# The first of four layers written as one unrolled, software-pipelined program instead of a loop over pairs of batches

## The chip, the cores and the metric

One core of a Trainium2 chip. The metric is the device time of one execution in microseconds (us), median of several runs.

## The reference

Eight batches of 512 tokens with 128 channels pass through four layers: a Performer layer (attention by random features, and a feed-forward part), a rotary causal attention layer with a mixture of experts, a second attention layer, and a routed feed-forward layer. Only the first is touched here. With a layer norm before it and a residual after it, it computes for each batch:

```python
q, k, v = split(video @ Wq.T + bq), split(video @ Wk.T + bk), split(video @ Wv.T + bv)   # 16 heads of 8
# features of q and k, xp = (x * norm) @ proj.T, 32 a head:
#   ratio * (exp(xp - diag - stab) + EPS_K); stab is the maximum over a token's features (queries)
#   or over all tokens and features of the head (keys); diag is half the squared length, scaled
k_sum = jnp.sum(kp, axis=2)
denom = jnp.einsum('bhnm,bhm->bhn', qp, k_sum)
ctx = jnp.einsum('bhnm,bhnd->bhmd', kp, v)
out = jnp.einsum('bhnm,bhmd->bhnd', qp, ctx) / denom[..., None]
x = layer_norm(video + out @ Wo.T + bo, g2, be2)
return layer_norm(x + relu(x @ W1.T + b1) @ W2.T + b2, g3, be3)
```

## The kernel before

Every tensor of a batch lies with 128 tokens on the partitions, as four tiles (T = 4), or transposed with channels on the partitions. The whole X (8 batches) stays in SBUF. The function performer_layer writes one program for each engine, and semaphores join them. The programs are loops over four steps (the last step is written out behind a loop of three), and a step handles two batches, the lanes L = 0 and 1. Each lane owns four of the eight PSUM banks.

A step goes in this order, each part for both lanes before the next: y (the normalised input) is transposed and multiplied by wq, wk and wv; ScalarE (ACT) keeps q and k and their squares; PE sums the squares (hsel) to half lengths, which are transposed to dg. The keys' features are multiplied out tile by tile (L508, L518); VectorE (DVE) takes the maximum of each head (L329), and ACT copies the tile from PSUM to kp in SBUF (L443). GpSimd (POOL) takes the maximum over the partitions with partition_all_reduce (L251). The queries' features (L525) get their maxima (L340), the shift (L349) and the exponential (L448). Then the keys in SBUF are shifted (L358) and exponentiated (L451). EPS_K is added to both by POOL for lane 0 (L257, L261) and by DVE for lane 1 (L292). PE forms contexts and key sums with 32-column products on four groups of columns (L538), turns the queries' features, and multiplies (L561). DVE divides (reciprocal L370, product L372), adds the residual, norms (L72, L76, L78, L101) with the inverse root on POOL (L239), scale and shift (L314, L316); feed-forward products L576 and L581; two more norms. DVE writes all four normalisations itself (L101, L302).

In the loop the waits are against registers, and some instructions are preceded by a semaphore increment of passed that carries the wait:

```python
pool.wait_ge(km_ready[L], i + 1)
pool.sem_inc(passed, 1)
nc.gpsimd.partition_all_reduce(stab[L][:], km[L][:], P, RMAX).then_inc(stab_ready[L], 1)
```

SyncE issues the layer's loads and 65 writes of pads that a later layer needs. The next layer's first loads and its work begin when all engines have left this layer's block.

Of the kernel before, what the change touches and what calls it, by code (L numbers as in the profile page):

```python
# [18 lines left out]
M = 32  # L19
# [111 lines left out]
def performer_layer(nc, X, ident, w, consts, padded):  # L131


    ctx = ExitStack()
    with ctx:
        sems = []

        def sem(name):
# [4 lines left out]
        sb2 = lambda name, shape, dt=F32: [sb(f"{name}{L}", shape, dt) for L in range(LANES)]  # L143
        sem2 = lambda name: [sem(f"{name}{L}") for L in range(LANES)]

        banks = [[ctx.enter_context(nc.psum_tensor(f"pf_bank{L}{i}", [P, 512], F32)) for i in range(4)]
                 for L in range(LANES)]

        wq, wk, wv, wo = (sb(n, [P, D]) for n in ("wq", "wk", "wv", "wo"))
        w1 = sb("w1", [P, F])  # L150
        w2 = sb("w2", [P, FC, D])
        bq, bk = sb("bq", [P, 1]), sb("bk", [P, 1])
        b1 = sb("b1", [P, FC])
        bv, bo, b2, g2, be2, g3, be3 = (sb(n, [P, D]) for n in ("bv", "bo", "b2", "g2", "be2", "g3", "be3"))
        feats = sb("feats", [P, H * M])
        hsel = sb("hsel", [P, 32])
        bmask = sb("bmask", [P, P])
        ones = sb("ones", [P, 32])
        half = sb("half", [P, T])
        stats, mv, rstd = sb2("stats", [P, T, 6]), sb2("mv", [P, T, 2]), sb2("rstd", [P, T])  # L160
        y, yb, yT = sb2("y", [P, T, D]), sb2("yb", [P, T, D]), sb2("yT", [P, S])
        qT, kT, sqq, sqk = (sb2(n, [P, S]) for n in ("qT", "kT", "sqq", "sqk"))
        v = sb2("v", [P, T, D])
        dgT, dg = sb2("dgT", [64, S]), sb2("dg", [P, T, 64])
        kmx, km, stab = sb2("kmx", [P, T, H]), sb2("km", [P, H]), sb2("stab", [P, H])
        ck, qmx, cq = sb2("ck", [P, T, H]), sb2("qmx", [P, T, H]), sb2("cq", [P, T, H])
        kp, qp = sb2("kp", [P, T, H * M]), sb2("qp", [P, T, H * M])
        cm, cx = sb2("cm", [P, 2, P]), sb2("cx", [P, 2, P])
        qpT = sb2("qpT", [P, T, S])
        rd, oT = sb2("rd", [P, S]), sb2("oT", [P, S])  # L170
        r, x1, x1b, x1T = sb2("r", [P, T, D]), sb2("x1", [P, T, D]), sb2("x1b", [P, T, D]), sb2("x1T", [P, S])
# [30 lines left out]
        def ahead(i):  # L202

            return 0 if isinstance(i, int) else 1

        def steps(eng, body):

            with eng.Fori(0, STEPS - 1) as i:
                body(i)
# [2460 lines left out]
```

## Time and profile before

| | |
|---|---|
| median of 3 runs | 1964.24 us (1961.62 to 1968.32) |
| the profiled execution's own time | 1969.18 us |
| its span | 1967.4 us |
| mean granted TensorE clock over the span | 0.873 of full |
| PE, DVE, ACT, POOL busy | 78%, 69%, 51%, 39% of the span |

The profile is one execution of the program. PE is the matmul engine, PEld its weight loads. Busy shares are over the whole span, of which the first layer is about a fifth; a row about a stage is read from the trace with a window. A matmul of 32-bit operands leaves two records.

### The profile page before, as it was taken

Reading aid. Unit: us, or ns where it says so; the run is one execution under the profiler, and the core shown is the slowest. Engines: PE = TensorE matmul, PEld = TensorE weight load, DVE = VectorE, ACT = ScalarE, POOL = GpSimd, SP = SyncE. Lnnn points to the kernel's source line nnn. Section 1 sums busy time; section 2 is a strip of 40 time slices with the busy share of each in tenths; the row PEclk is TensorE's granted clock in tenths of the full one; section 3 lists DMA queues with packets and bytes.
Section 4 is the critical chain, followed back from the end, with each engine's and each line's share of the span. In section 5 each row is a group of like instructions: output and inputs, shape, how many; then the busy total and the mean of one; then the engine's idle time right before and its main releaser. Section 6 shows DMA issues by size and latency. Waiting matters only on the chain. (4 is left out here: it accounts for less than half of the span.)

```text
span 1967.4 us, 26210 instructions
## 1 busy us (share of the span) xinstructions
PE 1537.9 (78%) x8477; PEld 972.8 (49%) x8477; DVE 1349.8 (69%) x3332; ACT 993.9 (51%) x1645; POOL 758.6 (39%) x871
## 2 busy tenths in 40 slices
PE   5475757537999999968737999999999478699990
PEld 2343434324666666633314555555554456577770
DVE  4557676746677777725867777887784465588874
ACT  3232323211565666532442667777776434477772
POOL 1121222214455555332555112212200357488875
PEclk9687878765899999978966999999999589799995
DMA  7500000013222222100006543444440011344424
GB/s 227 197 0 0 0 0 0 1 37 93 68 68 70 70 70 70 33 12 0 1 6 159 133 111 90 121 123 122 116 96 14 23 51 47 117 134 127 133 62 129
DMA packets 96189, 144.20 MB, mean 73 GB/s; under 512 B 31138, under 2 KB 59939, under 8 KB 91952
## 3 DMA queue, kind: packets, MB, share of 16 engines
q1 hardware_dynamic: 91072, 134.18, 24.3%
q0 software_dynamic: 4992, 8.48, 1.3%
q8 instruction: 63, 1.03, 0.2%
q14 instruction: 62, 0.51, 0.1%
HBM read 104.25 MB, written 57.48 MB: 82 GB/s over the span
## 5 line engine op out<-in xcount | busy, mean ns | idle before, releaser
L1010 DVE TENSOR_REDUCE ctx_nm<-ctx_s 128x1 f32<-128x512 f32 x512 | 329.5, 681 | 95.1 <-PE ctx_s L1286 94.4
L1122 ACT ACTIVATE ctx_probs<-ctx_st 128x1024 f32<-128x1024 f32 x256 | 254.2, 1022 | 113.6 <-PE ctx_st L1302 109.3
L1010 DVE TENSOR_REDUCE rope_nm<-rope_s 128x1 f32<-128x128 f32 (+3 forms) x512 | 230.4, 481 | 88.1 <-PE rope_s L1289 85.6
L1122 ACT ACTIVATE rope_probs<-rope_st 128x1024 f32<-128x1024 f32 (+1 forms) x256 | 172.3, 702 | 141.4 <-PE rope_st L1302 140.4
L1286 PE MATMUL ctx_s<-ctx_kst,ctx_qst 96*128 96x512 f32 x512 | 219.7, 467 | 17.2 <-DMA ctx_kst<-ctx_contexts 8.2
L1286 PE MATMUL rope_s<-rope_kst,rope_qst 96*128 96x128 f32 (+3 forms) x512 | 186.2, 396 | 4.4 <-DVE rope_nm L1010 3.6
L1302 PE MATMUL ctx_st<-ctx_qst,ctx_kst 98*128 98x512 f32 x512 | 164.7, 404 | 2.3 <-ACT ctx_probs L1122 2.3
L1286 PEld LDWEIGHTS ctx_s<-ctx_kst,ctx_qst 96*128 96x128 f32 x512 | 100.3, 196 | 131.0 <-DVE ctx_nm L1010 54.9
L875 POOL TENSOR_SCALAR_AFFINE_SELECT rope_probs<-rope_probs 128x256 f32<-128x256 f32 x256 | 98.3, 409 | 172.5 <-ACT rope_probs L1122 172.0
L1302 PE MATMUL rope_st<-rope_qst,rope_kst 98*128 98x512 f32 (+3 forms) x512 | 141.7, 360 | 3.9 <-ACT rope_probs L1122 3.9
L2476 DVE TENSOR_TENSOR sw_hf<-sw_silu,sw_u 128x512 f32<-128x512 f32 x124 | 84.6, 682 | 85.5 <-ACT sw_silu L2246 52.6
L2246 ACT ACTIVATE sw_silu<-sw_g 128x512 f32<-128x512 f32 x124 | 74.2, 598 | 121.0 <-PE sw_g L109 96.4
L2482 DVE TENSOR_TENSOR sw_hl<-sw_hf,sw_hh 128x512 fp32r<-128x512 f32 x124 | 128.6, 1037 | 0.1
L1318 PE MATMUL ctx_out<-ctx_probs,ctx_vaug 128*32 128x512 f32 x1024 | 123.8, 602 | 0.2 <-ACT ctx_probs L1122 0.2
L1286 PEld LDWEIGHTS rope_s<-rope_kst,rope_qst 96*128 96x128 f32 x512 | 104.4, 204 | 34.5 <-issue 17.6
L1289 PE MATMUL rope_s<-rope_maskb,rope_identb 128*128 128x128 bf16 x512 | 120.6, 240 | 0.0
L2335 POOL DMA_INDIRECT sw_ys<-sw_yo,sw_xin x92 | 104.2, 1132 | 29.1 <-issue 23.8
L1302 PEld LDWEIGHTS ctx_st<-ctx_qst,ctx_kst 98*128 98x128 f32 x512 | 97.7, 193 | 24.0 <-ACT ctx_probs L1122 6.9
L239 POOL TENSOR_TENSOR pf_rstd<-pf_mv,pf_half 128x4 f32<-128x4 f32 x32 | 33.0, 1031 | 194.9 <-DVE pf_mv L78 194.9
L1302 PEld LDWEIGHTS rope_st<-rope_qst,rope_kst 98*128 98x128 f32 x512 | 92.3, 201 | 14.4 <-ACT rope_probs L1122 5.9
L2318 POOL TENSOR_TENSOR sw_wl<-sw_raw,sw_wh 128x1536 fp32r<-128x1536 f32 x24 | 84.1, 3504 | 36.7 <-ACT sw_wh L2224 36.7
L1318 PE MATMUL rope_out<-rope_probs,rope_vaug 128*32 128x512 f32 (+3 forms) x1024 | 84.4, 449 | 3.0 <-POOL rope_probs L875 3.0
(380 smaller groups left out, 3346.8 us busy)
## 6 DMA issues: line engine op xcount, KB each, us to landing
sw_raw<-in_L_ffn_all SPq DMA_DIRECT2D x24, 768.0 KB
sw_xs<-in_pad SPq DMA_DIRECT2D x65, 260.0 KB, 9.4
rope_halves<-rope_qk SPq DMA_DIRECT2D x24, 512.0 KB
ctx_halves<-ctx_qk SPq DMA_DIRECT2D x24, 512.0 KB, 6.0
ctx_qst<-ctx_contexts SPq DMA_DIRECT2D x32, 384.0 KB
ctx_kst<-ctx_contexts SPq DMA_DIRECT2D x32, 384.0 KB
rope_qst<-rope_halves SPq DMA_DIRECT2D x32, 192.0 KB
rope_kst<-rope_halves SPq DMA_DIRECT2D x32, 192.0 KB
```

Of the source, the lines that this page charges most:

```text
L875: last = nc.gpsimd.affine_select(blocks, blocks, [[0, 2], [1, P]], compare_op=ALU.is_ge, fill=0.0, base=0, channel_multiplier=-1)
L1010: nc.vector.tensor_reduce(nm[:, g, j * T + t:j * T + t + 1], bank("s", b, n)[:, 0:keys], AXX, ALU.max, negate=True).then_inc(s_used, 1)
L1122: nc.scalar.activation(probs[n // GH % 2][:, n % GH, u * units[0]:u * units[0] + units[u]], st_bank[u][:, 0:units[u]], ACT.Exp, scale=SCAL ...
L1286: last = nc.tensor.matmul(out[:, 0:keys], qst[0:KS, g, j, t * P:(t + 1) * P], kst[0:KS, g, j, 0:keys], start=True, stop=not causal)
L1289: last = nc.tensor.matmul(out[:, keys - P:keys], identb[:], maskb[:], start=False, stop=True)
L1302: last = nc.tensor.matmul(st_bank[u][:, lo:lo + width[c]], kst[:, g, j, c * P:(c + 1) * P], qst[:, g, j, S - width[c]:S], start=True, stop ...
L1318: last = nc.tensor.matmul(o_bank[32 * j:32 * j + 32, S - width[c]:S], vaug[g // 2][:, s, c, j, :], probs[s][:, j, at(c):at(c) + width[c]], ...
L2246: nc.scalar.activation(silu[m % 2][:], g_bank[m % 2][:], ACT.Silu).then_inc(silu_ready, 1)
L2318: nc.gpsimd.tensor_tensor(wl[s % WR][:], raw[s % 2][:], wh[s % WR][:].bitcast(F32), ALU.subtract).then_inc(wl_ready, 1)
L2335: nc.gpsimd.indirect_dma_start(ys[:, :], bass.IndirectOffsetOnAxis(ap=where_to, axis=0), yo[j % YR][:, t, :], None, bounds_check=2 * B * S ...
L2476: nc.vector.tensor_tensor(hf[m % 3][:], silu[m % 2][:], u_bank[m % 2][:], ALU.mult).then_inc(hf_ready, 1)
L2482: nc.vector.tensor_tensor(hl[m % RING][:], hf[m % 3][:], hh[m % RING][:].bitcast(F32), ALU.subtract).then_inc(hl_ready, 1)
```

## The change

The loop over pairs of batches becomes a straight program over 13 rounds. In round b the engines work on different stages of up to six batches: main part m = b, input part f = b+1, input norm f2 = b+2, division and first norm a = b-1, feed-forward e = b-2, last two norms g = b-3. Most buffers are single or doubled rings. Eight PSUM banks are divided anew: four (held) keep a batch's key features from the product to the shift, so that the shift reads PSUM and writes kp (no copy by ACT), and serve between for the contexts, numerator, denominator and both feed-forward products; two rings of two (brief) serve all else, each claimed in an order fixed by IN_ROUND. The keys' and queries' EPS_K and ratio leave the elementwise work: queries' by the bias of the copy out of PSUM, keys' by extra products of v with a constant tile floor and by EPS_K * S in the mask. v's bias moves into mask_contexts. The four normalisations move to ACT (scale and bias operands, whose bias nb is a small DVE operation, offsets); the scales and shifts by g2, be2, g3, be3 and the squares of q and k move to POOL. The reciprocal and its product (divide) of batch b-1 stand on DVE behind the first two maxima of the keys of batch b.

Core of the diff (removed lines are in the kernel printed above):

```diff
+        held = [ctx.enter_context(nc.psum_tensor(f"pf_held{k}", [P, 512], F32)) for k in range(T)]
+        RB = 2
+        brief = {who: [ctx.enter_context(nc.psum_tensor(f"pf_{who}{k}", [P, 512], F32)) for k in range(RB)] for who in ("dve", "act")}
+        rounds = range(-2, B + 3)
+        IN_ROUND = {"dve": [("wo", 1, 1), ("qx", 0, T)],
+                    "act": [("x1T", 2, 1), ("yT", -1, 1), ("q", -1, 1), ("k", -1, 1), ("v", -1, 1), ("dg", -1, 1), ("dgt", -1, 1),
+                            ("qpT", 0, T), ("cx", 0, 1)]}
+        FOR_W2, FOR_CM, FOR_NUM, FOR_DEN = range(4)
...
+            def key_features(m, t):                                   # PE
...
+                if t == FOR_W2 and m >= 3:
+                    pe.wait_ge(r2_ready, m - 2)
+                if t == FOR_CM and m:
+                    pe.wait_ge(cm_ready, m)
+                if t == FOR_NUM and m:
+                    pe.wait_ge(oT_ready, m)
+                if t == FOR_DEN and m:
+                    pe.wait_ge(rd_ready, m)
+                nc.tensor.matmul(held[t][:], tile(kT[m % 2], t), feats[:], start=True, stop=True).then_inc(kx_ps, 1)
...
+            def contexts(m):
...
+                for t in range(T):
+                    for g in range(4):
+                        nc.tensor.matmul(dst[32 * g:32 * g + 32, 0:P], left(t, g), kp[:, t, g * P:(g + 1) * P], start=t == 0, stop=False)
+                        nc.tensor.matmul(dst[32 * g:32 * g + 32, 0:P], left(t, g), floor[:], start=False, stop=t == T - 1)
+                for t in range(T):
+                    for g in range(4):
+                        last = nc.tensor.matmul(dst[32 * g:32 * g + 32, P:2 * P], ones[:], kp[:, t, g * P:(g + 1) * P], start=t == 0, stop=t == T - 1)
...
+            def widen(e):
+                pe.wait_ge(x1T_ready, e + 1)
+                for c in range(FC):
+                    if e + 2 < B:
+                        pe.wait_ge(kx_used, (e + 2) * T + c + 1)
...
+                    nc.tensor.matmul(held[c][:], tile(w1, c), x1T[:], start=True, stop=True).then_inc(h_ps, 1)
...
+            # PE's round: key_features 0, 1; turn_x1(e); turn_input(f); key_features 2, 3; output(a); query_features 0, 1;
+            # project(f); query_features 2, 3; widen(e); lengths(f); turn_lengths(f); contexts(m); turn_queries(m);
+            # turn_contexts(m); narrow(e); attend(m)
...
+            def largest_key(m):                                       # POOL
+                pool.wait_ge(km_ready, m + 1)
+                nc.gpsimd.partition_all_reduce(stab[:], km[:], P, RMAX).then_inc(stab_ready, 1)
...
+            for b in rounds:
+                m, f, f2, a, g = b, b + 1, b + 2, b - 1, b - 3
+                if within(m):
+                    largest_key(m)
+                if within(g):
+                    inverse_root(2, g)
+                if within(f):
+                    squares(f)
+                if within(g):
+                    affine2(g)
+                if within(a):
+                    inverse_root(1, a)
+                if within(f2):
+                    inverse_root(0, f2)
+                if within(g):
+                    inverse_root(3, g)
+                if within(a):
+                    affine1(a)
+                if within(f2):
+                    with_bias(f2)
...
+            def offsets(k, c):                                        # DVE
+                dve.wait_ge(rstd_ready[k], c + 1)
+                nc.vector.scalar_tensor_tensor(nb[k][:, c], mv[k][:, c, :, 0], -1.0, rstd[k][:, c], ALU.mult, ALU.mult).then_inc(nb_ready[k], 1)
...
+            def divide(a):
+                dve.wait_ge(nd_ps, 2 * a + 2)
+                nc.vector.reciprocal(rd[:], held[FOR_DEN][:]).then_inc(rd_ready, 1)
+                dve.wait_ge(rd_ready, a + 1)
+                if a:
+                    dve.wait_ge(wo_ps, a)
+                nc.vector.tensor_tensor(oT[:], held[FOR_NUM][:], rd[:], ALU.mult).then_inc(oT_ready, 1)
...
+            def shift_keys(m):
+                dve.wait_ge(stab_ready, m + 1)
...
+                    nc.vector.tensor_tensor(feat(kp[:, t, :]), feat(held[t][:]), each(ck[:, t, :], M), ALU.subtract).then_inc(kx_used, 1)
...
+            # DVE's round: with_x1(g); largest_keys(m) 0, 1; divide(a); spread(2); largest_keys(m) 2, 3; moments(2);
+            # with_input(a); shift_queries(m, 0); offsets(2); shift_keys(m); spread(1); shift_queries(m, 1); moments(1);
+            # spread(0, f2); offsets(1); moments(0); spread(3); offsets(0); mask_contexts(m); moments(3); offsets(3); residual(g)
...
+            # ACT's round: keep_x1(e); keep_input(f); keep_projected(f); query_exponents(m, 0); normalise(2, g);
+            # key_exponents(m); rectify(e); query_exponents(m, 1); keep_lengths(f); place_lengths(f); input_norm(f2);
+            # keep_queries(m); normalise(1, a); keep_contexts(m); normalise(3, g)
```

In the diff the three rounds that stand here as comments are written as calls, in that order. spread is the statistics (bn_stats) of four tiles, moments their aggregation and the addition of EPS. claim on PE waits until the bank two claims earlier in the same ring has been emptied.

## Rows read from the trace of the kernel before

**Rows 1.** Timeline, where the first layer starts and ends: start, duration, instructions [idle before].
```profile
5.58 0.87 DVE L72 BATCH_NORM_STATS2 pf_stats<-X 128x6 f32<-128x128 f32 x4 [5.58 <-PEq L2572]
...
15.50 1.28 ACT L431 ACT_TABLE_LOAD   x1 [15.50 <-DMA pf_bv<-in_L_attn_bv]
...
428.96 1.29 DVE L405 TENSOR_TENSOR X<-X,pf_r 128x512 f32<-128x512 f32 x2
```

**Rows 2.** Windows, third step: length, busy of PE, PEld, DVE, ACT, POOL, clock, DMA.
```profile
210.76:309.93 99.17, 61.64 (x382) 37.43 (x381) 67.92 (x166) 30.53 (x46) 21.80 (x17) 0.81 0.00 0
```

**Rows 3.** Waits of DVE, then of PE, in the same step: us, times, longest.
```profile
DVE pf_r L390 <- PE pf_bank L581: 9.4, 2, 6.5
DVE pf_dg L324 <- PE pf_bank L513: 5.5, 1, 5.5
...
PE pf_bank L508 <- DVE pf_v L320: 10.6, 1, 10.6
```

**Rows 4.** Lines by form, DVE, 0 to 430.3 us; L349, L72, L76 also by timeline.
```profile
L370 DVE RECIPROCAL pf_rd<-pf_bank 128x512 f32<-128x512 f32 x8 | 26.8, 3353 | 17.1 <-PE pf_bank L561 17.1
L101 DVE TENSOR_SCALAR pf_x<-pf_r,pf_mv,pf_rstd 128x128 f32<-128x128 f32 x64 | 17.8, 342 | 1.7 <-POOL pf_rstd L239 1.7
L314 DVE TENSOR_TENSOR pf_x<-pf_x,pf_g 128x512 f32<-128x512 f32 x16 | 11.0, 689 | 0.3
...
249.68 2.48 DVE L349 TENSOR_TENSOR pf_qp<-pf_bank,pf_cq 128x512 f32<-128x512 f32 x4
...
423.49 0.86 DVE L72 BATCH_NORM_STATS2 pf_stats<-pf_x 128x6 f32<-128x128 f32 x4
424.50 0.38 DVE L76 BATCH_NORM_AGGREGATE pf_mv<-pf_stats 128x2 f32<-128x6 f32 x4 [0.15 <-DVE pf_stats L72]
```

**Rows 5.** Timeline, ACT and POOL: single instructions that carry the sums.
```profile
151.47 2.25 ACT L448 ACTIVATE pf_qp<-pf_qp 128x1024 f32<-128x1024 f32 x2 [4.60 <-DVE pf_qp L349]
...
227.41 2.47 POOL L246 TENSOR_TENSOR pf_yb<-pf_y,pf_bo 128x512 f32<-128x512 f32 x2
...
302.43 4.15 ACT L470 ACTIVATE pf_hT<-pf_bank,pf_b 128x512 f32<-128x512 f32 x7 [2.69 <-PE pf_bank L576]
...
426.67 1.03 POOL L239 TENSOR_TENSOR pf_rstd<-pf_mv,pf_half 128x4 f32<-128x4 f32 x1 [0.50 <-DVE pf_mv L78]
...
440.90 1.65 ACT L1082 ACTIVATE Y<-X,rope_nb,rope_rstd 128x128 f32<-128x128 f32 x4 [33.07 <-DMA rope_bv<-in_L_ffn_bv]
```

**Rows 6.** Timeline around the all-reduce: steps 1 and 2, and its end in step 4.
```profile
37.48 0.42 DVE L333 TENSOR_REDUCE pf_km<-pf_kmx 128x16 f32<-128x64 f32 x2
49.21 0.78 POOL L251 PARTITION_ALL_REDUCE pf_stab<-pf_km  x2 [20.51 <-issue]
61.22 1.04 POOL L257 TENSOR_SCALAR pf_qp<-pf_qp 128x1024 f32<-128x1024 f32 x1 [11.23 <-issue]
...
146.16 0.42 DVE L333 TENSOR_REDUCE pf_km<-pf_kmx 128x16 f32<-128x64 f32 x2
152.52 0.78 POOL L251 PARTITION_ALL_REDUCE pf_stab<-pf_km  x2 [22.73 <-issue]
160.00 2.15 POOL L257 TENSOR_SCALAR pf_qp<-pf_qp 128x1024 f32<-128x1024 f32 x2 [6.70 <-issue]
...
358.58 4.21 POOL L257 TENSOR_SCALAR pf_qp<-pf_qp 128x1024 f32<-128x1024 f32 x2 [6.97 <-ACT pf_qp L448]
```

**Rows 7.** Timeline of PE in the third step.
```profile
233.35 5.53 PE L508 MATMUL pf_bank<-pf_feats,pf_kT 128*128 128x512 f32 x8 [10.61 <-DVE pf_v L320]
244.88 3.60 PE L525 MATMUL pf_bank<-pf_feats,pf_qT 128*128 128x512 f32 x8
268.80 1.08 PE L538 MATMUL pf_bank<-pf_kp,pf_v 128*32 128x128 f32 x32 [1.13 <-POOL pf_kp L261]
```

**Rows 8.** Windows of the L508 and the L525 work of rows 7.
```profile
233.00:239.00 6.00, 5.65 (x11) 2.38 (x12) 0.80 (x2) 0.00 (x0) 0.00 (x0) 0.66 0.00 0
245.00:250.00 5.00, 3.47 (x9) 1.21 (x7) 3.97 (x10) 1.14 (x2) 0.00 (x0) 1.00 0.00 0
```

More of the change, by code:

```diff
@@ L156, in performer_layer @@
[L156 to L165, printed above, removed]
@@ new lines, in shift_queries @@
+            def shift_queries(m, pair):
+                for t in (2 * pair, 2 * pair + 1):
+                    dve.wait_ge(qx_ps, m * T + t + 1)
+                    last = nc.vector.tensor_reduce(qmx[:, t, :], feat(bank("qx", m, t)[:]), AXX, ALU.max)
+                ch.do(last)
+                ch.sync()
+                dve.wait_ge(dg_ready, m + 1)
+                ch.do(nc.vector.tensor_tensor(cq[:, both(pair)], qmx[:, both(pair)], dg[m % 2][:, both(pair), 0:H], ALU.add))
+                ch.sync()
+                for t in (2 * pair, 2 * pair + 1):
+                    if m and t == 0:
+                        dve.wait_ge(qpT_ps, m * T)
+                    nc.vector.tensor_tensor(feat(qp[:, t, :]), feat(bank("qx", m, t)[:]), each(cq[:, t, :], M), ALU.subtract).then_inc(qx_used, 1)
@@ new lines, in residual @@
+            def residual(g):
+                dve.wait_ge(n3_ready, g + 1)
+                x = X[:, g * T:(g + 1) * T, :]
+                nc.vector.tensor_tensor(x, x, x3[:], ALU.add).then_inc(done, 1)
+            for b in rounds:
+                m, f2, a, g = b, b + 2, b - 1, b - 3
+                if b == -1:
+                    dve.wait_ge(projected, 16 * H)
+                    nc.vector.tensor_scalar_mul(feats[:], feats[:], DH ** -0.25).then_inc(feats_ready, 1)
+                if within(g):
+                    with_x1(g)
+                if within(m):
+                    largest_keys(m, (0, 1))
+                if within(a):
+                    divide(a)
+                if within(g):
+                    spread(2, r2)
+                if within(m):
+                    largest_keys(m, (2, 3))
+                if within(g):
+                    moments(2, g)
+                if within(a):
+                    with_input(a)
+                if within(m):
+                    shift_queries(m, 0)
+                if within(g):
+                    offsets(2, g)
+                if within(m):
+                    shift_keys(m)
+                if within(a):
+                    spread(1, r)
+                if within(m):
+                    shift_queries(m, 1)
+                if within(a):
+                    moments(1, a)
+                if within(f2):
+                    if f2 == LANES:
+                        dve.wait_ge(x_loaded, 16)
+                    spread(0, X[:, f2 * T:(f2 + 1) * T, :])
+                if within(a):
+                    offsets(1, a)
+                if within(f2):
+                    moments(0, f2)
+                if within(g):
+                    dve.wait_ge(x2_ready, g + 1)
+                    spread(3, x2)
+                if within(f2):
+                    offsets(0, f2)
+                if within(m):
+                    mask_contexts(m)
+                if within(g):
+                    moments(3, g)
+                    offsets(3, g)
+                    residual(g)
```

726 lines of the change are left out of this document (368 added, 358 removed).

## The prediction

> **What bounds the kernel now.** I read the page first: four layers stand one behind another in the span, and the diff touches only the first (all names with pf_). The timeline's ends give its place: its first DVE instruction starts at 5.58 us, its weights let ACT and PE start at 15.50, its last residual starts at 428.96 and ends at 430.25 [rows 1]. The rest of the span, 1,537 us, runs the same code before and after; the change moves it to an earlier or later start and nothing else, as the next layer's loads start only when this one has ended. So the sum is made for 430.3 us.
>
> Next the windows: a step of the loop (two batches) lasts 99.2 us; DVE is busy for 67.9 of them, PE 61.6, ACT 30.5, POOL 21.8, the granted clock 0.81 [rows 2]. No engine is full. The table of waits says why: DVE waits 9.4 us for the second feed-forward product and 5.5 for the lengths; PE waits 10.6 us for DVE before the key features [rows 3]. The two batches of a step move in lock step through a chain DVE to PE to ACT, and where one engine works the others stand. The bound is latency, 49.6 us a batch, with DVE as the largest worker (34.0 a batch).
>
> **What the change does to each engine's work.** Per batch in the new program:
>
> DVE. A 512-wide operation that reads PSUM takes 0.69 us, and four in a row 2.48, so 0.62 apiece. There are 20 (four key maxima, four query maxima, eight shifts, oT, the sums with_input, with_x1 and residual): 12.4. Reciprocal 3.35. Sixteen statistics at 0.28 alone, four in 0.86: 3.4; sixteen aggregates (four in 0.38) 1.5; and sixteen small ones (masks, epsilon, offsets, sums over heads), for which I take 0.2 each, between a 0.1 aggregate and a 0.28 statistic: 3.1. Sum 23.8 us [rows 4]. Gone are the affine pairs (their first halves alone took 11.0 us over eight batches), all four normalisations (two of them 17.8), the two additions of EPS_K over 2048 columns, v's bias and the copy of dg [rows 4]: 34.0 becomes 23.8.
>
> ACT. It inherits the normalisations: the next layer's own one, four instructions of 128 columns, takes 1.65 us; four of them 6.6. Sixteen copies and Relus of 0.6 to 0.7 make 9.7, four exponentials of 1024 columns 4.2 [rows 5]. About 20.6 us: not a bound.
>
> POOL. Four inverse roots of 1.03, and eight 512-wide sums and products of 1.25 (squares two, affine1 three, affine2 two, yb one): 14.2 us [rows 5]. Then the all-reduce, and here the rows say more than its 0.43 us. In the second step the key maxima end at 146.58, the two all-reduces start at 152.52 and end at 153.30, 6 us after the first maximum although POOL had been idle for 22.7 us, and the second costs only 0.4 more: a fixed price in front. The next POOL instruction had its data from ACT since 152.6 and starts at 160.00, 6.7 us after the all-reduces. In the fourth step the way back is 7.0; in the first the two gaps are 11.5 and 11.2 [rows 6], while SyncE's queue was issuing the pads. So going to the all-reduce costs about 6.1 us and coming back about 6.8. The Trainium skill (GPSIMD Engine Reference, 2.1 Instruction dispatch) says that the first call to a freshly loaded Q7 kernel pays a code load of about 6 us that has no instruction in the profile; by that page alone one load for each change of library would cost what the row shows, and it speaks against this change, which makes eight such trips instead of four. In the sum: POOL 14.2+0.4+6.1+6.8 = 27.5 us a batch, now the largest worker.
>
> PE. At full clock a 512-column product costs 0.85 (eight records of the query features in 3.60 with the last one's tail) [rows 7]. Sixteen of them (features 8, projections 2, widen 4, attention 8 that run four at a time and cost 2) are 13.7; the 128-column products, four in 0.86: v, wo and four groups of narrow, 5.2; seven groups of four transposes 3.0; hsel 0.9; contexts 0.9 for v and 0.9 for ones. The new products with floor repeat v's: 0.9 if four column groups still overlap. About 25.5 us.
>
> **The round, which sets the time.** No worker fills 49.6, so I walk one steady round (b from 3 to 7), from T = 0, when divide has written oT of batch b-1. Each step is a duration above. Held bank 2 is free: key product 2 to 1.1, product 3 to 2.0, their maxima to 2.7, km at 3.0. The all-reduce runs at once if its code is already loaded: stab 3.5. POOL comes back at 10.2, inverse_root(2) ends 11.3. DVE meanwhile does moments(2), with_input, shift_queries(0) to 7.7, and then stands in offsets(2) until 11.3: a new stall of 3.6 us, since that small operation is queued before shift_keys, whose stab has long been there. POOL's round begins with the wait for km, and behind it are queued inverse_root(2), squares(f), on which PE's lengths and contexts wait, and all other roots. No DMA is added or moved on any queue. shift_keys to 14.1, shift_queries(1) to 17.6. PE waits with widen for each shifted key tile, to 15.9; ACT's rectify and second query exponent to 18.7, dgT and dg behind them 20.3, contexts on PE from 19.8 to 22.5. The masks to 23.5, moments(3), POOL and offsets(3) to 25.3. ACT has the input norm to 23.0, four qpT copies 25.5, normalise(1) 27.2, cx 27.6, normalise(3) 29.3, so residual ends at 30.0. PE ends narrow at 29.5 and attend at 31.3. The next round: key products 0 and 1 to 33.1, the second maximum 33.7, reciprocal and oT 37.8, which is the next T. The reciprocals' move costs nothing by itself: after the first two maxima DVE has nothing else that is ready, and the next key products wait for the banks that divide empties.
>
> So 38 us a round at full clock. PE stands still for 4 us at the divide; before, after 10.6 us of standing four key products took 5.53 us and four query products, after work without a gap, 3.60 [rows 7]; the granted clock was 0.66 (part at 1.2 GHz, part at 2.4) in the stretch with the first and 1.00 in that with the second [rows 8]. I add 1.5: 39.5. POOL is idle from 32.4 and its load for the next all-reduce (6.1) ends at 38.5, before the next km at 42.5: hidden.
>
> Ends. The pads' traffic stays. Round 0 starts at 20.5 as before; its km comes about 28.5, POOL is back 11.2 later [rows 6], its squares(1) hold PE's contexts(0): T of round 1 about 58. Rounds 1 and 2 have no third norm and last 29 each: 116. Five rounds of 39.5: 314. The drain has no key work: output, norm 1, widen and narrow of batch 7, its two last norms behind those of batch 6, in DVE's order: about 42. The layer ends at 356 instead of 430.3: 74 us less. The profiled execution took 1969.2 (span 1967.4), 5 above the median of 1964.2; the difference is the same for both, so 1964-74 = 1890.
>
> **Rivals.**
> (a) The code load waits with the all-reduce. The rows can't exclude it: before, a signal stood between wait and all-reduce, and the load ran behind it; in the new program nothing does, so I take the load as free to run early. If it isn't, stab and all behind it come 6.1 us later in each round that has one, and POOL's return moves to 17.3, so DVE stalls nearly 10 us in offsets(2): 5 times 6.1 and some 7 in rounds 1 and 2, 37 us: 1927.
> (b) The products with floor don't overlap. Each stands directly behind the product with the same 32 columns of the array; before, neighbours were always on other columns, and 32 records took 1.08 us [rows 7], no row shows the new order. If the next column group starts only with the last of four passes of 0.107 (a quarter of a 512-column record), 16 pairs take 5.1 in place of 1.8, some 3.3 to 4.2 us a round on the path contexts, masks, norm 3: 8 rounds, 30 us: 1920. The Trainium skill (TensorE: Matmul & The Clock Gate, Part 3, The mechanism) says that matmuls are a strict queue without reordering; by it this case would hold, though the trace's L538 rows show two passes of each product overlapping in fours.
> (c) It is slower. Each all-reduce pays the first step's price, 11.5 and 11.2, fully on DVE's path: a round is 38+6.1+9.8 = 54, and 130+5x54+42 = 442, 12 us later: 1976. It decides from 51 a round. Against it: the second and the fourth step show 6.7 and 7.0 back [rows 6], and the fourth is straight-line code as the new program is.
> (d) It packs better: the drain overlaps, rounds of 36: 1865.
>
> **Numbers.** The forecast 0.62 (my range 1870 to 1910), (a) 0.14, (b) 0.13, (c) 0.04, (d) 0.07. The walk has some 40 hand-offs, each perhaps 0.1 late, so errors lean up: the range is 1860 to 1930. A measurement here tells 0.3% (6 us) from no change. Faster 0.94, same 0.02, slower 0.04.
>
> **What would show it.** The last pf residual near 356. DVE's wait in offsets(2) for POOL of 3 to 4 us in rounds 3 to 7 (about 10: rival a), with the all-reduce within 1 us of km. POOL's next instruction 6.8 us after each all-reduce. L538's successor, 64 records for v and floor, in 2 us (5 or more: rival b). Reciprocals without PE waiting long before them. The forecast is wrong if POOL's return is not hidden at all or doesn't happen, or if ACT's strict order (four norms between the copies) holds qpT back.

## The result and the profile after

On the chip that timed both, the changed kernel took 1942.11 us (median of 4 runs, 1934.17 to 1942.89) beside 1965.24 (1961.62 to 1968.32) for the kernel before: ratio 0.9874, 95% interval 0.9843 to 0.9905. So it is faster, by 1.3%, which is clear of the 0.3% that a measurement tells from no change, and outside the predicted range: the forecast had 74 us, of which 23 came, a third.

The layer's end is the sharper measure, since the rest of the program runs unchanged code, and that rest is not constant: it took 1537.2 us in the profile before and 1527.6 in the one after, so that 9.5 of the 35.0 us between the two spans have nothing to do with the layer. Timeline of DVE, its last line in the layer:

```profile
404.09 0.69 DVE L578 TENSOR_TENSOR X<-X,pf_x 128x512 f32<-128x512 f32 x1 [1.71 <-ACT pf_x L636]
```

It ends at 404.78 instead of 430.25 [rows 1]: 25.5 us earlier, where 356 was forecast; 48.8 us are missing. Timeline of POOL, the eight all-reduces (one a round), which give the rounds' length:

```profile
46.62 0.39 POOL L419 PARTITION_ALL_REDUCE pf_stab<-pf_km  x1 [11.11 <-issue]
84.06 0.40 POOL L419 PARTITION_ALL_REDUCE pf_stab<-pf_km  x1 [17.78 <-DVE pf_km L520]
121.36 0.40 POOL L419 PARTITION_ALL_REDUCE pf_stab<-pf_km  x1 [10.16 <-DVE pf_km L520]
157.26 0.40 POOL L419 PARTITION_ALL_REDUCE pf_stab<-pf_km  x1 [10.15 <-DVE pf_km L520]
201.75 0.39 POOL L419 PARTITION_ALL_REDUCE pf_stab<-pf_km  x1 [10.06 <-DVE pf_km L520]
245.99 0.40 POOL L419 PARTITION_ALL_REDUCE pf_stab<-pf_km  x1 [10.06 <-DVE pf_km L520]
290.19 0.40 POOL L419 PARTITION_ALL_REDUCE pf_stab<-pf_km  x1 [10.06 <-DVE pf_km L520]
332.26 0.40 POOL L419 PARTITION_ALL_REDUCE pf_stab<-pf_km  x1 [10.83 <-DVE pf_km L520]
```

The forecast had the first at 28.5, the next three at 61, 90 and 119, then one every 39.5, and 79 from the last to the end. So the first is 18.1 us late, the next three intervals (37.4, 37.3, 35.9) are 4.9, 8.3 and 6.9 too long, the four steady ones (44.5, 44.2, 44.2, 42.1) 17.0 together, and the tail (72.5) is 6.5 short: 48.7. Five places, then, not one.

Windows of one steady round (length, busy of PE, PEld, DVE, ACT, POOL, clock), which answers to [rows 2] for half a step:

```profile
201.75:245.99 44.24, 33.57 (x224) 19.16 (x224) 26.08 (x70) 19.61 (x36) 14.41 (x13) 0.85 0.00 1
```

The work of three engines came near the forecast (in brackets): ACT 19.6 (20.6), POOL 14.4 (14.2 and 0.4), DVE 26.1 (23.8). PE's 33.6 are well above the 25.5 that I had at full clock; the clock was 0.85 here, and a round of the best version below, at 1.00, has 28.7. No engine is full all the same, and what was furthest off is the waiting. Waits from 215 to 262, which answer to [rows 3]:

```profile
POOL pf_rstd L415 <- issue: 7.0, 1, 7.0
DVE pf_nb L501 <- POOL pf_rstd L415: 5.6, 4, 3.8
...
PE pf_held L362 <- DVE pf_kp L530: 4.4, 1, 4.4
...
PE pf_held L263 <- DVE pf_oT L509: 3.9, 1, 3.9
```

Timeline of DVE in that round; the lines of [rows 6] are answered by 245.59 here, 245.99 above and 253.36 below:

```profile
232.16 1.41 DVE L578 TENSOR_TENSOR X<-X,pf_x 128x512 f32<-128x512 f32 x1 [4.07 <-ACT pf_x L636]
233.50 0.68 DVE L572 TENSOR_TENSOR pf_r<-pf_held,pf_x1b 128x512 f32<-128x512 f32 x1
235.52 1.48 DVE L514 TENSOR_REDUCE pf_kmx<-pf_held 128x16 f32<-128x512 f32 x2 [1.35 <-PE pf_held L263]
236.92 3.35 DVE L505 RECIPROCAL pf_rd<-pf_held 128x512 f32<-128x512 f32 x1
240.30 0.69 DVE L509 TENSOR_TENSOR pf_oT<-pf_held,pf_rd 128x512 f32<-128x512 f32 x1
...
245.59 0.26 DVE L520 TENSOR_REDUCE pf_km<-pf_kmx 128x16 f32<-128x64 f32 x1
...
254.45 1.01 DVE L501 SCALAR_TENSOR_TENSOR pf_nb<-pf_mv,pf_rstd 128x4 f32<-128x4 f32 x1 [3.76 <-POOL pf_rstd L415]
255.38 1.14 DVE L525 TENSOR_TENSOR pf_ck<-pf_dg,pf_stab 128x64 f32<-128x64 f32 x1
256.56 2.48 DVE L530 TENSOR_TENSOR pf_kp<-pf_held,pf_ck 128x512 f32<-128x512 f32 x4
```

The same stretch on POOL:

```profile
231.75 1.28 POOL L440 TENSOR_TENSOR pf_x<-pf_x,pf_be 128x512 f32<-128x512 f32 x1
...
253.36 1.05 POOL L415 TENSOR_TENSOR pf_rstd<-pf_mv,pf_half 128x4 f32<-128x4 f32 x1 [6.98 <-issue]
254.41 1.03 POOL L426 TENSOR_TENSOR pf_sqq<-pf_qT 128x512 f32<-128x512 f32 x1
255.41 1.03 POOL L426 TENSOR_TENSOR pf_sqk<-pf_kT 128x512 f32<-128x512 f32 x1
257.22 1.27 POOL L448 TENSOR_TENSOR pf_x<-pf_x,pf_g 128x512 f32<-128x512 f32 x1 [0.78 <-ACT pf_x L636]
```

And on PE:

```profile
213.37 6.49 PE L362 MATMUL pf_held<-pf_x1T,pf_w 128*128 128x512 f32 x8 [4.66 <-DVE pf_kp L530]
...
222.51 0.45 PE L309 MATMUL pf_held<-pf_kp,pf_v 128*32 128x128 f32 x8
222.75 0.42 PE L310 MATMUL pf_held<-pf_floor,pf_v 128*32 128x128 f32 x8
...
224.28 1.13 PE L313 MATMUL pf_held<-pf_kp,pf_ones 128*32 128x128 f32 x32
...
234.32 1.96 PE L263 MATMUL pf_held<-pf_feats,pf_kT 128*128 128x512 f32 x4 [0.19 <-DVE pf_r L572]
...
241.05 3.78 PE L263 MATMUL pf_held<-pf_feats,pf_kT 128*128 128x512 f32 x4 [3.90 <-DVE pf_oT L509]
```

Read together: the all-reduce starts 0.14 us after km has ended, so nothing was left to load in between (the code that the all-reduce needs, called its library below), and POOL's next instruction starts 6.98 us behind it; DVE waits 3.76 in offsets(2). All three were forecast. Not forecast: two key products take 1.96 us at 234.32 and 3.78 at 241.05, behind 3.90 us of standing; eight records of widen take 6.49 behind 4.66 us of standing, where eight of the query features took 3.60 [rows 7]; and three DVE operations (1.41, 1.01, 1.14) take two to six times what they take elsewhere in the layer (0.69, 0.16, 0.22).

Each ratio below has the kernel before timed beside it (1952.6 to 1953.8 there), with its 95% interval. A steady round is half the distance between km or the all-reduce of batch 4 and batch 6; in the changed kernel 44.2.

A layer end is read from one profile, and it is only good to some 6 us. Two kernels below ("keys shifted before offsets(2)" and "both moves") have the changed kernel's code in every round up to the all-reduce of batch 3. It starts at 157.26 us in the changed kernel, at 160.21 in the first of them, and in the second at

```profile
163.17 0.39 POOL L419 PARTITION_ALL_REDUCE pf_stab<-pf_km  x1 [9.86 <-DVE pf_km L520]
```

The load ahead of the first all-reduce took 11.1, 10.9 and 13.7 us in the three, and the way back from it 10.4, 12.5 and 12.2. So a gain of a few us counts only where it arises behind the edit, in rows that the edit explains; the 22 to 35 us of the copy, the divide first and the maximum by PE stand clear of this.

### The profile page after: what moved, and what is told of

It is laid out like the page before. It is cut to its first block and busy times, and to the rows that moved or that the text cites. A ratio compares the mean times of both kernels' runs of the same rounds, so it can differ in the third digit from the quotient of the medians.

```text
span 1932.4 us, 26699 instructions
## 1 busy us (share of the span) xinstructions
PE 1551.3 (80%) x8728; PEld 973.5 (50%) x8733; DVE 1282.8 (66%) x3212; ACT 1026.0 (53%) x1747; POOL 792.7 (41%) x909
## 5 line engine op out<-in xcount | busy, mean ns | idle before, releaser
L1444 PEld LDWEIGHTS rope_s<-rope_kst,rope_qst 96*128 96x128 f32 x512 | 103.7, 203 | 33.6 <-issue 16.9
L2485 POOL DMA_INDIRECT sw_xs<-sw_rows,sw_slots x64 | 66.9, 1046 | 47.0 <-issue 35.6
```

Of the source, the lines that this page charges most:

```text
L1444: last = nc.tensor.matmul(out[:, 0:keys], qst[0:KS, g, j, t * P:(t + 1) * P], kst[0:KS, g, j, 0:keys], start=True, stop=not causal)
```

## Experiments

**A copy for the all-reduce.** A copy of km on POOL replaces it, so the maximum over the partitions is left out.

```diff
-                nc.gpsimd.partition_all_reduce(stab[:], km[:], P, RMAX).then_inc(stab_ready, 1)
+                nc.gpsimd.tensor_copy(stab[:], km[:]).then_inc(stab_ready, 1)
```

> The changed kernel with a plain copy of km to stab in place of the all-reduce: the maximum over the partitions is left out. Theory 1 (the way back from the all-reduce, 7.0 us with 10.4 in round 0, holds offsets(2) and squares on POOL, and DVE and PE behind them): POOL's next operation follows within 0.2 us, DVE's wait of 3.8 us in offsets(2) is gone, a steady round falls from 44.2 to about 39, the first rounds lose some 17 and twice 3 us, in all 45 to 55 us less than the changed kernel. Theory 2 (the round is set by hand-offs and PE's clock, POOL's pause is mostly hidden): only the first round's 17 us and under 1 us a round, so 17 to 25 us less.

Ratio 0.9673 (0.9641 to 0.9704), layer end 369.46, steady round 38.6. Timeline of POOL:

```profile
223.24 0.20 POOL L419 COPY pf_stab<-pf_km 128x16 f32<-128x16 f32 x1 [9.78 <-DVE pf_km L520]
223.75 1.02 POOL L415 TENSOR_TENSOR pf_rstd<-pf_mv,pf_half 128x4 f32<-128x4 f32 x1 [0.31 <-DVE pf_mv L497]
```

The 6.98 us behind the all-reduce are gone. The trips cost the layer 35.3 us: 11.7 up to the maximum of batch 1; 5.0, 6.5, 4.8 and 3.0 in the four intervals after batch 3 (5.6 in the steady round); and 4.8 in the tail. Not all of it is DVE's wait: with POOL back early, widen follows without a gap and takes 3.60 us, and ck takes 0.21. The intervals between batches 1, 2 and 3 hardly move (37.6 and 36.1 beside 37.3 and 35.9), so the loads are not what is wrong there.

**The same copy in the kernel before**, the maximum over partitions left out again.

> The kernel before with plain copies of km to stab in place of the all-reduces: the maximum over the partitions is left out. Theory 1 (before, the code loads lay beside the queries' exponents, which come at the same time): a step stays at 99.2 us within 1, only the first step gains its cold load, the layer ends 5 to 12 us earlier, so that the loads of the changed kernel (35 us there) are a cost that the change itself put on the path. Theory 2 (they were on the path before too): each step loses 6 us or more, the layer ends 25 us or more earlier.

Ratio 0.9983 (0.9968 to 0.9997), layer end 428.41: 1.8 us earlier. That is a net of two parts. The keys' maxima of step 2 end 8.8 us earlier (137.75 beside 146.58), but the two steps behind them take 103.9 and 102.4 us instead of 99.5 and 99.0, where theory 1 had them unchanged; TensorE was busy for 66.3 us of the first of these instead of 61.7, at a clock of 0.77 instead of 0.79, and why is open. What the run does show is that taking the all-reduces out brought next to nothing before and brings 35 us now. Timeline of POOL in step 2, its first instruction behind the two copies:

```profile
143.97 1.04 POOL L257 TENSOR_SCALAR pf_qp<-pf_qp 128x1024 f32<-128x1024 f32 x1 [5.86 <-ACT pf_qp L448]
```

Even with nothing to come back from, POOL stands for 5.86 us until ACT has the queries' exponentials; before, the way back of 6.7 us [rows 6] lay beside this wait. The change put inverse_root(2), for which DVE waits, and the squares behind the all-reduce, and their inputs are there before POOL is back (inverse_root(2) starts 0.31 us after them in the run above).

**Keys shifted before offsets(2).** On DVE alone.

```diff
                 if within(m):
                     shift_queries(m, 0)
-                if within(g):
-                    offsets(2, g)
                 if within(m):
                     shift_keys(m)
+                if within(g):
+                    offsets(2, g)
```

> The changed kernel with offsets(2) behind shift_keys on DVE instead of ahead of it. Theory 1 (a small operation queued ahead holds the shift): the shift starts as soon as the queries are shifted, 4 to 6 us earlier against the next divide, DVE waits about 1 us in offsets(2), a steady round is 3 to 4 us shorter, in all 12 to 20 us less. Theory 2 (POOL's return or ACT's order sets the round anyway: normalise(2) stands ahead of the key exponents on ACT and waits for the same offset): the key exponents start when they did and the time changes by less than 5 us.

Ratio 0.9847 (0.9808 to 0.9886), layer end 403.8. From batch 3's all-reduce, where the edit begins to act, to the end it takes 243.6 us instead of 247.5: 3.9 us, where theory 1 had 12 to 20, and less than the 5.9 by which the same stretch differs on unchanged code in the run with bo's own semaphore below. The keys' shift starts 4.9 us after km instead of 10.7, and widen runs at 3.60 us, but ACT's list still has normalise(2) ahead of the keys' exponentials. Timeline of ACT, then of PE:

```profile
255.40 1.65 ACT L636 ACTIVATE pf_x<-pf_r,pf_nb,pf_rstd 128x128 f32<-128x128 f32 x4 [2.41 <-DVE pf_nb L501]
...
262.81 0.66 PE L295 MATMUL pf_act<-ident,pf_dgT 64*128 64x64 f32 x4 [5.27 <-ACT pf_dgT L669]
263.40 0.67 PE L309 MATMUL pf_held<-pf_kp,pf_v 128*32 128x128 f32 x8
```

The gap moves from before widen to before the contexts, which now take 0.67 where they took 0.45.

**Both moves, DVE and ACT**: offsets(2) behind shift_queries(1), normalise(2) behind query_exponents(1).

> The changed kernel with offsets(2) behind shift_queries(1) on DVE and normalise(2) behind the second query exponent on ACT, so that neither stands ahead of the keys. Theory 1 (the order of both engines together held the keys): the key shift starts about 4 us earlier, the exponents and rectify with it, a round is 3 to 4 us shorter, 15 to 25 us in all. Theory 2 (POOL's return sets squares, lengths and so contexts, and the last norm's chain sets the end of the round): the keys are earlier and the round is the same within 1 us.

Ratio 0.9867 (0.9848 to 0.9887), layer end 411.11. A steady round gets 2.7 us shorter (41.5), yet the layer is 6.3 us longer. Of these, 5.9 arise ahead of batch 3's all-reduce, where nothing was changed (163.17 beside 157.26). Behind it the four intervals win 9.3 us (165.7 instead of 175.0) and the tail gives back 9.8 (82.3 instead of 72.5): the last round's norm 2 and all behind it come later, and DVE waits 9.2 us there for POOL's inverse root where it waited 4.0. So the two moves win nothing on balance, which is neither theory. A single stall is not what holds the layer; where one is filled, the work moved behind it waits elsewhere.

**bo with a semaphore of its own.** POOL's with_bias(0) waits for all eleven late loads, ahead of squares(0); here it waits for bo alone, and affine1(0) takes over the wait for the rest.

```diff
+            sp.dma_start(bo[:], w["bo"]).then_inc(bo_loaded, 16)
             for dst, src in loads:
...
                 if c == 0:
-                    pool.wait_ge(loaded, 16 * len(loads))
+                    pool.wait_ge(bo_loaded, 16)
```

> The changed kernel with a semaphore of its own for bo, so that with_bias(0) on POOL does not wait for all eleven loads. Theory: with_bias(0) held squares(0) behind it and PE idle for 8 us; now squares(0) starts by 20 us instead of 26.7, the first keys' maxima end about 8 us earlier than 40.3, and the layer ends 6 to 8 us earlier. Rival: the first all-reduce's code load (11 us, starts behind with_bias(1)) sets round 0, and moves too since with_bias(1) moves with it; if the load waits for something else, under 3 us is won.

Ratio 0.9818 (0.9779 to 0.9857), layer end 397.2: 7.6 us earlier, most of which is not the edit's. Timeline of POOL in the changed kernel, then in this one:

```profile
25.46 1.26 POOL L434 TENSOR_TENSOR pf_yb<-pf_y,pf_bo 128x512 f32<-128x512 f32 x1 [17.06 <-DMA pf_be<-in_L_attn_be]
26.68 1.04 POOL L426 TENSOR_TENSOR pf_sqq<-pf_qT 128x512 f32<-128x512 f32 x1
...
34.24 1.27 POOL L434 TENSOR_TENSOR pf_yb<-pf_y,pf_bo 128x512 f32<-128x512 f32 x1 [4.55 <-ACT pf_y L636]
```

```profile
22.02 1.04 POOL L428 TENSOR_TENSOR pf_sqq<-pf_qT 128x512 f32<-128x512 f32 x1
...
41.44 0.39 POOL L421 PARTITION_ALL_REDUCE pf_stab<-pf_km  x1 [10.59 <-issue]
```

The squares, on which the first lengths and so all of round 0 wait, start at 22.02 instead of 26.68; km ends at 34.14 instead of 40.26, 6.1 us earlier, and the first all-reduce starts 5.2 us earlier. At batch 3's only 1.7 are left, as the first way back took 12.5 us instead of 10.4. The other 5.9 of the 7.6 us arise in the four steady intervals (169.1 instead of 175.0), whose code is the same in both. Timeline of PE there:

```profile
237.27 1.98 PE L265 MATMUL pf_held<-pf_feats,pf_kT 128*128 128x512 f32 x4 [3.90 <-DVE pf_oT L513]
...
252.08 5.37 PE L364 MATMUL pf_held<-pf_x1T,pf_w 128*128 128x512 f32 x8 [4.91 <-DVE pf_kp L534]
```

Behind gaps as long as in the changed kernel, two key products take 1.98 us instead of 3.78, and widen 5.37 instead of 6.66: in this profile the clock was back sooner (0.92 and 0.93 in the rounds from 198.39 and 240.41, instead of 0.85), and no edit in these rounds explains it.

POOL's rows show the start's second loss: the load for the first all-reduce begins only when with_bias(1) has ended (35.5 in the changed kernel) and takes 11.1 us there, 10.6 here, so the all-reduce stands 6.4 us behind a km that had ended at 40.26.

**PE kept at work.** Products that nobody reads: four ahead of key products 2 and 3, five ahead of widen.

```diff
+                if within(a) and within(m):
+                    busy(claim("wo", a), 4)                       # nc.tensor.matmul(dst[:], ident[:], feats[:]), four times
                 if within(m):
                     key_features(m, 2)
                     key_features(m, 3)
...
+                if within(f) and within(m):
+                    busy(claim("dg", f), 5)
                 if within(e):
                     widen(e)
```

> The changed kernel with products of ident and feats that nobody reads, four into the bank of the output product before key products 2 and 3, five into the bank of the lengths before the first feed-forward product, in the two places where PE stood for 3.9 and 4.7 us a round. Theory 1 (the granted clock falls in those gaps and costs about 1.7 us at the keys and 2.5 at the feed-forward product a round): key products 2 and 3 take 2.0 instead of 3.8 us, the feed-forward's four 3.8 instead of 6.5, a steady round is 3 to 4.5 us shorter, 25 to 35 us in all. Theory 2 (what PE loses is hidden behind POOL's return and ACT's queue): the products get shorter and the round by less than 1.5 us, under 10 us in all.

Ratio 0.9818 (0.9766 to 0.987), layer end 397.2, steady round 40.4. Timeline of PE:

```profile
198.76 1.98 PE L263 MATMUL pf_held<-pf_feats,pf_kT 128*128 128x512 f32 x4 [0.47 <-DVE pf_oT L517]
...
208.50 4.45 PE L374 MATMUL pf_act<-pf_feats,ident 128*128 128x512 f32 x10
213.28 3.67 PE L362 MATMUL pf_held<-pf_x1T,pf_w 128*128 128x512 f32 x8 [0.32 <-DVE pf_kp L538]
```

Two products back to 1.98 and widen to 3.67, in every steady round: measured against this profile of the changed kernel, the drops of the clock behind the two gaps cost 3.8 us a steady round (against the profile of the run before it, whose clock came back sooner, 1.7). The four intervals win 11.7 us; 7.6 remain, since the all-reduce of batch 3 comes 4.0 us later than in the changed kernel. Of these, 3.5 are there at the first all-reduce already, behind a load of 13.6 us instead of 11.1, so that the products are in the way in rounds 0 to 2 is not shown.

**The divide first.** DVE takes the reciprocals of batch b-1 before the maxima of batch b's keys. This undoes the one part of the change that is an order chosen on DVE alone.

```diff
+                if within(a):
+                    divide(a)
                 if within(m):
                     largest_keys(m, (0, 1))
-                if within(a):
-                    divide(a)
```

> The changed kernel with divide ahead of the first two key maxima on DVE instead of behind them. Theory 1 (the place behind the maxima costs): numerator and denominator are there when with_x1 ends, so the reciprocal starts some 2.6 us earlier, key products 2 and 3 come earlier by as much, and a round is 2 to 4 us shorter, 15 to 30 us in all. Theory 2 (as forecast, the reciprocals' place costs nothing): DVE waits for the numerator before divide for as long as it waited for key products, and the time is within 5 us of the changed kernel's.

Ratio 0.9724 (0.9706 to 0.9743), layer end 382.56, steady round 40.4. Timeline of DVE, then of PE:

```profile
222.21 0.68 DVE L572 TENSOR_TENSOR pf_r<-pf_held,pf_x1b 128x512 f32<-128x512 f32 x1
222.97 3.36 DVE L505 RECIPROCAL pf_rd<-pf_held 128x512 f32<-128x512 f32 x1
...
230.25 0.26 DVE L520 TENSOR_REDUCE pf_km<-pf_kmx 128x16 f32<-128x64 f32 x1
...
227.11 1.98 PE L263 MATMUL pf_held<-pf_feats,pf_kT 128*128 128x512 f32 x4 [1.25 <-DVE pf_oT L509]
```

In the changed kernel the reciprocal starts 2.74 us after with_x1 has ended (236.92 against 234.18), here 0.08. The divide needs only what PE's attend has already left in its banks; the two maxima wait for products that PE starts after with_x1. PE's gap shrinks from 3.90 to 1.25, and the two key products behind it stay at full speed: 2.7 from the order and 1.8 from the clock, partly given back to POOL's later return (offsets(2) waits 4.14 instead of 3.76).

**The maximum over partitions by PE and DVE**, whole: PE transposes km, DVE takes the maximum of each row and sets it on a diagonal, PE multiplies it by ones to all partitions, DVE copies it. POOL never leaves its common operations.

```diff
+            def largest_key(m):                                  # PE, behind output(a)
+                dst = claim("st", m)
...
+                nc.tensor.transpose(dst[0:16, 0:P], km[:], ident[:]).then_inc(turned_km, 1)
+                pe.wait_ge(diagonal, m + 1)
+                nc.tensor.matmul(dst[:, P:P + 16], across[:], diag[:], start=True, stop=True).then_inc(spread_km, 1)
...
+                ch.do(nc.vector.tensor_reduce(kc[:], bank("st", m)[0:16, 0:P], AXX, ALU.max))
+                ch.sync()
+                nc.vector.tensor_scalar(diag[:], ident[0:16, 0:16], kc[:], None, ALU.mult).then_inc(diagonal, 1)
```

> The changed kernel with the maximum over the partitions made by PE and DVE (transpose of km, a maximum, a diagonal, a product with ones, a copy) instead of POOL's all-reduce; it computes all that the reference does. Theory 1 (the code loads cost 35 us of the layer): the pauses on POOL are gone, the round costs 1 to 2 us for the two hand-offs and three small DVE operations on the path, so 39.5 to 41 us, and the layer ends 22 to 32 us earlier than the changed kernel's 404.8. Theory 2 (the hand-offs cost what the loads did): within 8 us of the changed kernel.

Ratio 0.9739 (0.9721 to 0.9756), layer end 380.43, steady round 39.9. It brings 24.4 of the 35.3 us. Here too widen stands without a gap and takes 3.60 us in the steady rounds.

**Narrow squares.** POOL's squares are taken over 8 of 512 columns; the rest holds ones, so nearly all lengths are left out.

```diff
-                    nc.gpsimd.tensor_tensor(dst[:], src[f % 2][:], src[f % 2][:], ALU.mult).then_inc(sq_ready, 1)
+                    nc.gpsimd.tensor_tensor(dst[:, 0:8], src[f % 2][:, 0:8], src[f % 2][:, 0:8], ALU.mult).then_inc(sq_ready, 1)
```

> The changed kernel with the squares of queries and keys taken over 8 columns in place of 512; the other columns hold ones, so the lengths of nearly all positions are not computed (left out). Theory 1 (VectorE's small operations are slowed by GpSimd's squares beside them): offsets(2) and the copy of the last half of the lengths go from 1.01 and 1.14 us back to 0.16 and 0.21, the keys' shift ends 1.8 us earlier, a steady round takes 42 to 42.5 us in place of 44.2, the layer ends 9 to 12 us earlier. Theory 2 (they are slow for another reason, as a wait that the row counts into them): both stay at 1 us and the layer ends within 3 us of the changed kernel's 404.8.

Ratio 0.981 (0.9791 to 0.9828), layer end 392.8, steady round 40.4. Timeline of DVE, the two operations that took 1.01 and 1.14:

```profile
247.72 0.17 DVE L504 SCALAR_TENSOR_TENSOR pf_nb<-pf_mv,pf_rstd 128x4 f32<-128x4 f32 x1 [3.95 <-POOL pf_rstd L415]
247.82 0.31 DVE L528 TENSOR_TENSOR pf_ck<-pf_dg,pf_stab 128x64 f32<-128x64 f32 x1
```

Theory 1 holds for the two operations: from the all-reduce's start to the keys' shift it is 8.97 us instead of 10.57. Widen takes 5.37 instead of 6.49 behind a shorter gap (2.90 to 3.21), but it took 5.37 behind 4.91 with bo's own semaphore, so this part isn't shown to be the edit's. The 3.8 us of the round are more than the collisions; the squares' own 2 us on POOL also went, so the run doesn't price the collision alone.

**Together, three versions.** First the divide first and bo's own semaphore:

> The divide ahead of the first two maxima and bo with a semaphore of its own, nothing else. Alone the two moved the end of the layer by -22.2 and -7.6 us against the changed kernel. Theory 1: the one acts in rounds 3 to 7 and the other ahead of round 0, so they add: the layer ends near 375 us, the ratio to the kernel before is about 0.969. Theory 2: the all-reduce's library load swallows the start's gain again: near 381, ratio 0.972.

Layer end 373.9, as theory 1 has it (375); the ratio is 0.9736 (0.9717 to 0.9755) where it had 0.969, no better than with the divide alone. In the two profiles the rest of the program took 1526 us here and 1515 there; it varies between 1515 and 1537 over all these kernels, and why is open. Then with the maximum by PE:

> The whole reduction across partitions by TensorE and VectorE, the divide first, bo with its own semaphore; nothing is left out. Theory 1: the three gains add (-24.4, -22.2, -7.6): the layer ends near 351, ratio about 0.960. Theory 2: the first two remove the same wait of a steady round, since each by itself ends at 39 to 40 us a round, so together they bring little more than one: steady rounds of 38 to 39 us, layer end near 368, ratio 0.968. I take a value between, 360, ratio 0.964.

Ratio 0.959 (0.957 to 0.9611), median 1873.56: 4.1% under the kernel before, and the best version. The layer ends at 353.1, near theory 1's 351 and earlier than the 360 that I took, with a steady round of 35.9. Timelines of PE and of DVE:

```profile
182.20 1.88 PE L271 MATMUL pf_dve<-pf_feats,pf_qT 128*128 128x512 f32 x4
183.92 3.60 PE L375 MATMUL pf_held<-pf_x1T,pf_w 128*128 128x512 f32 x8
...
187.00 1.28 DVE L559 TENSOR_TENSOR pf_cq<-pf_qmx,pf_dg 128x32 f32<-128x32 f32 x1
```

The two gaps were two waits, not one: the divide first closes the one ahead of the key products and leaves widen's (4.8 to 5.7 us there), the maximum by PE does the opposite. With both gone, widen follows the query features without a pause, and from 182 to 188 us the clock is 1.00 of full. Last, that version with the five unread products ahead of widen:

> As the run before, with five unread products on TensorE ahead of the widen products. Theory 1: the four widen products start after an idle time of over 4 us and take 6 us in place of 3.6, on the path of the contexts: -2 us a steady round, layer end 10 to 12 us earlier than in the run before. Theory 2: with the stabiliser made on TensorE the idle time ahead of the widen products is already gone, or the widen products are off the path: within 2 us of the run before.

Ratio 0.9633 (0.9614 to 0.9652), layer end 363.4, steady round 37.9: 10 us worse. Theory 1 was wrong. Theory 2 had it that no gap was left to fill, but not the price (within 2 us): the products (4.46 us) push widen back.

## Why the prediction was right in sign and wrong in size

**What held.** No engine fills a round; the round is a chain. The library's load in front of the all-reduce is hidden in a steady round, the way back is not, and DVE pays for it in offsets(2) with 3.76 us (forecast 3.6). Rival (a) is refuted: 0.14 us lie between km's end and the all-reduce in the rows of after. Rival (b) too: from 222.51 to 224.28, 64 records of v and floor take 1.77 us, less than twice the 1.08 of 32 [rows 7]. The Trainium skill's strict queue (TensorE: Matmul & The Clock Gate, Part 3, The mechanism) didn't cost this, though neighbours stand on the same columns. Rival (c) needed 51 us a round and got 44.2. The way back took 6.9 to 7.6 us from batch 3 on; of the rows that I read it from, the fourth step's 6.97 names ACT as what ended it [rows 6], so it was weaker support than I took it for. The tail from the last all-reduce was 6.5 us shorter than my 79, and that is luck, not skill: the term was too large, and hid as much of what the others below lacked.

**Step 1 that failed: "Round 0 starts at 20.5 as before; its km comes about 28.5"**, the start. It came at 40.3, and the all-reduce 6.4 later: 18.1 us. I walked round 0 by the durations of its work and didn't ask what stands at the head of POOL's list: with_bias(0), with a wait for eleven loads, ahead of squares(0). With a semaphore of its own for bo, km comes 6.1 us earlier. The load in front of the first all-reduce, which I put at nothing in round 0, is the 6.4. The other 5.7 stay open.

**Step 2: "Rounds 1 and 2 have no third norm and last 29 each"**. The three intervals up to batch 3 were 37.4, 37.3 and 35.9: 20 us in all, the largest part of what is missing. This was an estimate without a walk. As the rows read, a third norm's work lies beside the chain, which goes from oT through key products, shift, contexts, the turned queries and attend back to the divide, and is in every round. The divide first took 4 and 3 us from the second and third; with all three edits they are 34.5 and 34.0. That the loads lengthen the second and third is excluded by the copy's run (37.6 and 36.1); the first falls to 32.2 there, but its way back from the all-reduce (10.4 us) was in my walk with 11.2. The divide's place accounts for 7 of the 20 us; the rest is argued from the rows, not shown.

**Step 3: "I add 1.5" for the clock.** Two stretches drop, not one: key products 2 and 3 behind 3.90 us of standing (3.78 instead of 1.98) and widen behind 4.66 (6.49 instead of 3.60), and widen's is on the path to the contexts. Filling both gaps gives 3.8 us a round. Rows 7 and 8 showed the price; I placed it at one gap though my own walk had the other, PE waiting with widen for keys whose shift starts at 11.3. That second gap is POOL's way back again: in the runs without the all-reduce it is gone.

**Step 4: "The reciprocals' move costs nothing by itself: after the first two maxima DVE has nothing else that is ready"**. This asks what else is ready after the maxima, and not what is ready before them. The divide is. Its place costs 3.8 us a steady round and 22.2 us in the layer, in part through the clock of step 3, so the two do not add.

**Step 5: small DVE operations at 0.2 us.** (Sixteen of them are 3.2 us, not the 3.1 of my sum, which changes nothing.) The round has 0.85, 0.92 and 0.72 us more in nb, ck and the residual. All three read two tensors from SBUF while POOL runs a 512-wide operation; nb and ck end when POOL's does (255.46 beside 255.44, 256.52 beside 256.44), the residual 0.5 us behind it (233.57 beside 233.03). The keys' shift with one operand in PSUM shows nothing of it: 2.48 us beside POOL's product at 257.22, and 2.48 for the queries' in [rows 4]. The Trainium skill (GPSIMD Engine Reference, 1. Specifications) lists the SBUF interface as shared with VectorE, with contention for DVE instructions that have two SBUF inputs: the rows agree, and the change moved POOL's heavy work beside just such instructions.

The steady round is then 38 walked + 3.8 (clock) + 2.5 (collisions) = 44.3, measured 44.2, where the forecast had 38 + 1.5. The walk held in this kernel's order of operations, with the divide's place in it, and its surcharges were too low; the four intervals cost 17.0 of the 48.7. That the sum closes to 0.1 is partly luck, since the same code took 42.1 in the profile with bo's own semaphore.

## What to carry to other kernels

In a pipelined order, ask of each operation what is ready before its place, not only after: an operation with inputs long there behind one that waits for a product costs the difference twice, once as delay and once as the clock behind the other engine's gap. When work moves to an engine that makes trips of another kind (here an all-reduce), price its way back by what is now queued there: without its all-reduces the layer ended 1.8 us earlier before and 35.3 after. And walk the first rounds by the heads of the queues with their waits on loads; here the start and the first three intervals hold 38 of the 48.7 us that went missing. Before a few us between two profiles are explained, see what unchanged code varies by in them: 5.9 us here ahead of batch 3, and 5.9 again in four steady rounds.

## What was not expected of the hardware

A DVE operation over 4 columns took 1.01 us instead of 0.16 beside a POOL operation over 512, and one of 32 columns 1.28 instead of 0.19; beside POOL's squares over 8 columns they took 0.17 and (for 64 columns) 0.31. The load before the first all-reduce took 10.2 to 13.7 us in eight profiles, with DMA at 298 to 320 GB/s beside it in all of them, against 6 in a quiet stretch [rows 6]; the way back took 10.4 to 12.5 there, and 6.9 to 7.6 from batch 3 on in the changed kernel. And a gap of PE of 1.25 us left the two key products behind it at full speed (1.98), while behind one of 3.90 they took anything from 1.98 to 3.78.
